# Attention on one core: value products in halves of 256 columns, and one head's row maximum taken from half the keys plus a relu

## The reference, cut to what matters

```python
Q = (hs @ q_w + q_b).reshape(B, S, H, HD).transpose(0, 2, 1, 3)
K = (hs @ k_w + k_b).reshape(B, S, H, KPH).transpose(0, 2, 1, 3)
V = (hs @ v_w + v_b).reshape(B, S, H, KPH).transpose(0, 2, 1, 3)
scores = jnp.einsum('bhsk,bhtk->bhst', Q[..., :KPH], K) / math.sqrt(KPH)
attn = jax.nn.softmax(scores, axis=-1)
ao = jnp.einsum('bhst,bhtv->bhsv', attn, V)
```

## Time and profile before

| what | value |
|---|---|
| median of three executions | 4021.08 us |
| the profiled execution | 3990.48 us |
| its span, first to last instruction | 3988.9 us |
| mean granted TensorE clock | 0.922 of full speed |
| TensorE busy with products | 3377.5 us (85%) |
| VectorE busy | 3155.0 us (79%) |
| ScalarE busy | 2370.5 us (59%) |
| attention: first score product to last | 1926.56 to 3272.01 us |

### The profile page before, as it was taken

One profiled execution on the slowest core, in us unless ns is written; L12 is line 12 of the kernel. 1 busy time (PEld: TensorE's weight loads), 2 busy tenths in 40 slices (PEclk: granted clock), 3 DMA queues, 4 the chain that ended last, 5 costly groups with the idle time before them and its releaser, 6 DMA issues. The chain is left out here.

```text
span 3988.9 us, 64991 instructions
## 1 busy us (share of the span) xinstructions
PE 3377.5 (85%) x19711; PEld 2058.5 (52%) x19712; DVE 3155.0 (79%) x4214; ACT 2370.5 (59%) x4325; POOL 1366.7 (34%) x953
## 2 busy tenths in 40 slices
PE   8969898996669799797999999999999976299950
PEld 6745455553458688795333333333333324189940
DVE  7869999997866566477899999999999935277868
ACT  6668888886955433210577777777777761033323
POOL 7859998994014454301000000000000005744520
PEclk9989999998889899997799999999999996599975
DMA  7854444544869632394122323223223115222258
GB/s 262 283 187 164 159 163 166 179 146 166 280 174 255 164 111 74 109 291 134 27 54 62 69 53 72 58 55 75 54 60 71 30 21 178 87 86 89 90 175 293
DMA packets 531451, 521.11 MB, mean 131 GB/s; under 512 B 84784, under 2 KB 441264, under 8 KB 531040
## 3 DMA queue, kind: packets, MB, share of 16 engines
q1 hardware_dynamic: 517248, 480.45, 41.0%
q0 software_dynamic: 13952, 37.74, 2.7%
HBM read 301.15 MB, written 215.71 MB: 130 GB/s over the span
## 5 line engine op out<-in xcount | busy, mean ns | idle before, releaser
L2395 DVE TENSOR_REDUCE at_top<-at_psM 128x1 f32<-128x1024 f32 x1024 | 1205.1, 1218 | 101.5 <-PE at_psM L2254 99.8
L2363 ACT ACTIVATE at_probs<-at_psS 128x512 f32<-128x512 f32 x2048 | 1061.0, 603 | 286.0 <-PE at_psS L2280 286.0
L2280 PE MATMUL at_psS<-at_q,at_k 64*128 64x512 f32 x2048 | 803.4, 471 | 8.2 <-ACT at_probs L2363 8.1
L2254 PE MATMUL at_psM<-at_k,at_q 62*128 62x512 f32 x2048 | 704.9, 454 | 41.3 <-DMA at_vraw<-scratch_vf 22.0
L655 POOL TENSOR_TENSOR sc_prod<-sc_state,sc_c_row 128x1024 f32<-128x1024 f32 x256 | 648.8, 2564 | 84.1 <-DVE sc_state L806 72.2
L2254 PEld LDWEIGHTS at_psM<-at_k,at_q 62*128 62x128 f32 x2048 | 313.1, 190 | 621.4 <-DVE at_top L2395 539.3
L806 DVE TENSOR_TENSOR_SCAN sc_state<-sc_dec,sc_psI 128x1024 f32<-128x1024 f32 x256 | 574.2, 2276 | 43.6 <-PE sc_psI L727 34.0
L2293 PE MATMUL at_psV<-at_probs,at_v 128*32 128x512 f32 x4096 | 546.3, 605 | 0.0
L738 PE MATMUL sc_psY<-sc_prod,sc_ident 128*128 128x512 f32 x1024 | 480.5, 599 | 15.2 <-DVE sc_y L792 15.2
L2221 POOL COPY at_v<-at_vraw 128x256 f32<-128x256 f32 x32 | 12.8, 401 | 1249.4 <-DMA at_vraw<-scratch_vf 1166.6
L2280 PEld LDWEIGHTS at_psS<-at_q,at_k 64*128 64x128 f32 x2048 | 337.7, 184 | 170.3 <-ACT at_probs L2363 160.4
(11 more groups left out here) (409 smaller groups left out, 4904.4 us busy)
## 6 DMA issues: line engine op xcount, KB each, us to landing
sc_c_row<-scratch_bc SPq DMA_DIRECT2D x128, 512.0 KB, 3.7
scratch_xs<-at_zeros SPq DMA_DIRECT2D x140, 264.0 KB, 4.7
sc_b_row<-scratch_bc SPq DMA_DIRECT2D x32, 512.0 KB, 5.0
ec_y<-scratch_ys SPq DMA_DIRECT2D x32, 512.0 KB, 6.1
ex_x<-scratch_xs SPq DMA_DIRECT2D x39, 264.0 KB, 3.3
si_x<-in_x SPq DMA_DIRECT2D x16, 512.0 KB, 5.6
scratch_xn<-si_xn SPq DMA_DIRECT2D x16, 512.0 KB, 6.2
scratch_x_t<-si_xT SPq DMA_DIRECT2D x16, 512.0 KB, 3.1
```

Of the source, the lines that this page charges most:

```text
L2254: ins = pe.matmul(psM[t % 2][:, half * TILE:(half + 1) * TILE], rows_of(q4[j], h, 0, MAXROW)[:, c * P:(c + 1) * P], rows_of(k4[j], h, 0, M ...
L2280: pe.matmul(psS[v % 3][:], rows_of(k4[j], h, 0, GROUP)[:, c * P:(c + 1) * P], rows_of(q4[j], h, 0, GROUP)[:, half * TILE:(half + 1) * TILE ...
L2363: act.activation(probs[:, slot(j, v), :], psS[v % 3][:], ACT.Exp).then_inc(act_done, 1)
L2395: dve.tensor_reduce(top[j % 2][:, h, c:c + 1], psM[t % 2][:], AX.X, ALU.max, negate=True).then_inc(maxed, 1)
```

## The change

The value products of a group are cut into two halves of 256 columns, and one half is issued after each step in place of a whole group after every second one (`values`, `values_after`). Where a group is the last of its eight (`last_keys`), both halves are still issued together, after an odd step, and the even step behind it gets none.

Of the four heads of a quad, one (`DIFF_HEAD`, the tiles with t % 4 = 3) gets its row maximum in another way. With a the scores of a query against the first 512 keys and b those against the last 512, max(a, b) = b + relu(a - b). TensorE makes a - b in a `psS` bank with two accumulated products, against the first keys and against negated last keys `kn` (`difference`), two tiles ahead; ScalarE takes the relu of it into `mag` (`raised`); TensorE makes b alone in `psM`; VectorE adds the two and takes the maximum over 512 columns in one instruction (`tensor_tensor_reduce`, `maximum`). GpSimd negates the keys (`negative_keys`), once per unit. The entries of the `psS` banks are numbered ahead in one list, where a difference is an entry like a score: 9 entries for four steps instead of 8.

Besides, the clears of the operands are shared between VectorE (units 0 and 1) and GpSimd (2 and 3), the loads of a unit wait for that unit's clears alone, `ones` is cleared and copied later, `cleared.make` moves to the end of GpSimd's prologue, and loops of SP and GpSimd are written out.

The core of the diff:

```diff
-    turn_entry = TURN + 1
-    bank_at = dict(zip(at_slot, range(BANKS)))
-    NE = BANKS + 1
-    OPEN = 4
+    RING, PART = 24, TILE // 2
+    DIFF = 3
+    DIFF_HEAD = HEADS[DIFF]
+    score_at, diff_at, turn_at, entries = {}, {}, {}, 0
+    for v, t in [(0, t) for t in range(MT)] + [(1, t) for t in range(LEAD)]:
+        if t % QUAD == 1:
+            diff_at[v, t + 2], entries = entries, entries + 1
+    turn_at[0], entries = entries, entries + 1
+    for u in range(UNITS):
+        for s in range(MT):
+            for n in (2 * s, 2 * s + 1):
+                score_at[u, n], entries = entries, entries + 1
+                if n == TURN and u + 1 < UNITS:
+                    turn_at[u + 1], entries = entries, entries + 1
+            v, t = u + 1 + (s + LEAD) // MT, (s + LEAD) % MT
+            if v < UNITS and t % QUAD == 1:
+                diff_at[v, t + 2], entries = entries, entries + 1
     COLLECTED = (18 + LEAD, FIRST + LEAD)
...
+        kn = [m.sb(f"kn{j}", [MAXROW, TILE], F32R) for j in range(NQ)]
+        mag = [m.sb(f"mag{k}", [P, TILE]) for k in range(2)]
...
-                    sp.wait_ge(ready_made, 2 * j + 3)
+                    sp.wait_ge(zeroed[j], 2)
                     m.settle(sp)
                     load(0, j)
+                sp.wait_ge(ones_made, 1)
+                m.settle(sp)
+                for j in range(NQ):
                     for group in range(2):
                         dst = k4[j][GROUP * group + MAXROW:GROUP * (group + 1), :, :].bitcast(F32)
                         sp.dma_start(dst, ones[:]).then_inc(ones_in, 16)
...
-                cleared.make(pool)
+                for j in range(2, NQ):
+                    pool.memset(k4[j][:].bitcast(F32), 0.0).then_inc(zeroed[j], 1)
+                    pool.memset(q4[j][:].bitcast(F32), 0.0).then_inc(zeroed[j], 1)
...
+                def negative_keys(b, j):
+                    pool.wait_ge(loaded[j], (b + 1) * 16 * LOADS)
+                    pool.tensor_scalar(kn[j][:], rows_of(k4[j], DIFF_HEAD, 0, MAXROW)[:, TILE:T].bitcast(F32), -1.0, None,
+                                       ALU.mult).then_inc(kn_ready[j], 1)
...
-                def maxima(u, j, t, half):
-                    h, c = tile_of(t)
-                    if half == 0:
-                        if t > 1:
-                            pe.wait_ge(maxed, u * MT + (t - 1))
-                        elif not isinstance(u, int) or u:
-                            pe.wait_ge(maxed, u * MT + t - 1)
-                    ins = pe.matmul(psM[t % 2][:, half * TILE:(half + 1) * TILE],
+                def maxima(u, t, half):
+                    j, (h, c) = u % NQ, tile_of(t)
+                    if t % QUAD == DIFF and half == 0:
+                        return
+                    if half == (1 if t % QUAD == DIFF else 0) and u * MT + t > 1:
+                        pe.wait_ge(maxed, u * MT + t - 1)
+                    at = 0 if t % QUAD == DIFF else half
+                    ins = pe.matmul(psM[t % 2][:, at * TILE:(at + 1) * TILE],
                                     rows_of(q4[j], h, 0, MAXROW)[:, c * P:(c + 1) * P],
                                     rows_of(k4[j], h, 0, MAXROW)[:, half * TILE:(half + 1) * TILE], start=True, stop=True)
                     if half == NHALF - 1:
                         ins.then_inc(scored, 1)
...
+                def free(e):
+                    if e >= 3:
+                        pe.wait_ge(act_done, e - 2)
+                def difference(u, t):
+                    j, (h, c), e = u % NQ, tile_of(t), diff_at[u, t]
+                    free(e)
+                    pe.wait_ge(kn_ready[j], u // NQ + 1)
+                    query = rows_of(q4[j], h, 0, MAXROW)[:, c * P:(c + 1) * P]
+                    pe.matmul(psS[e % 3][:], query, rows_of(k4[j], h, 0, MAXROW)[:, 0:TILE], start=True, stop=False)
+                    pe.matmul(psS[e % 3][:], query, kn[j][:], start=False, stop=True).then_inc(keyed, 1)
...
-                def values(u, j, g):
-                    half, c = g // KC, g % KC
-                    pe.wait_ge(act_done, u * NE + (at_slot[4 * g + 3] + 2))
-                    if c == 0:
-                        pe.wait_ge(sums_ready, u * NHALF + (half + 1))
-                    if g == 0:
-                        pe.wait_ge(v_ready, u + (2 * NQ + 1))
+                def values(group, part):
+                    u, g = group // GROUPS, group % GROUPS
+                    j, half, c = u % NQ, g // KC, g % KC
+                    cols = slice(part * PART, (part + 1) * PART)
+                    if part == 0:
+                        pe.wait_ge(act_done, score_at[u, 4 * g + 3] + 1)
+                        if c == 0:
+                            pe.wait_ge(sums_ready, u * NHALF + (half + 1))
+                        if g == 0:
+                            pe.wait_ge(v_ready, u + (2 * NQ + 1))
                     for n, h in enumerate(KEYED):
-                        last = pe.matmul(psV[32 * h:32 * h + 32, :], v4[j][:, c, h, :], probs[:, slot(j, at_slot[4 * g + n]), :],
-                                         start=(c == 0), stop=(c == KC - 1))
-                    last.then_inc(summed, 1)
-                def step(u, j, b, s, last_unit, second_last):
-                    tile = s + LEAD
-                    ahead, t = 1 + tile // MT, tile % MT
-                    more = not (last_unit or (second_last and ahead == 2))
-                    mj, mb = (j + ahead) % NQ, b + (j + ahead) // NQ
+                        last = pe.matmul(psV[32 * h:32 * h + 32, cols], v4[j][:, c, h, :], probs[:, slot(u, 4 * g + n), cols],
+                                         start=(c == 0 and part == 0), stop=(c == KC - 1 and part == 1))
+                    if part == 1:
+                        last.then_inc(summed, 1)
+                def values_after(at):
+                    group = (at - 3) // 2
+                    if group < 0:
+                        return
+                    last_keys = group % KC == KC - 1
+                    if at % 2:
+                        values(group, 0)
+                    if at % 2 == 0 and not last_keys or at % 2 and last_keys:
+                        values(group, 1)
...
+                        scores(u, n)
+                        if n == TURN and u + 1 < UNITS:
+                            turn(u + 1)
+                    if more and t % QUAD == 1:
+                        difference(v, t + 2)
...
+                            pe.wait_ge(top_in[u % NQ], (u // NQ + 1) * 16 * QUAD)
+                        step(u, s)
+                        values_after(u * MT + s)
+                for at in range(UNITS * MT, UNITS * MT + 2):
+                    values_after(at)
...
+                def raised(u, t):
+                    e, k = diff_at[u, t], t // QUAD % 2
+                    act.wait_ge(keyed, e + 1)
+                    if u * MT + t >= 2 * QUAD:
+                        act.wait_ge(maxed, u * MT + t + 1 - 2 * QUAD)
+                    act.activation(mag[k][:], psS[e % 3][:], ACT.Relu).then_inc(act_done, 1)
...
-                dve.memset(ones[:], 1.0).then_inc(ready_made, 1)
-                for j in range(NQ):
-                    dve.memset(k4[j][:].bitcast(F32), 0.0).then_inc(ready_made, 1)
-                    dve.memset(q4[j][:].bitcast(F32), 0.0).then_inc(ready_made, 1)
-                dve.memset(top2[:], 0.0).then_inc(ready_made, 1)
...
+                for j in range(2):
+                    dve.memset(k4[j][:].bitcast(F32), 0.0).then_inc(zeroed[j], 1)
+                    dve.memset(q4[j][:].bitcast(F32), 0.0).then_inc(zeroed[j], 1)
+                dve.memset(ones[:], 1.0).then_inc(ones_made, 1)
+                dve.memset(top2[:], 0.0).then_inc(top2_made, 1)
...
+                def maximum(u, t):
+                    h, c = HEADS[t % QUAD], t // QUAD
+                    at = top[u % 2][:, h, c:c + 1]
+                    if t % QUAD != DIFF:
+                        dve.wait_ge(scored, u * MT + (t + 1))
+                        dve.tensor_reduce(at, psM[t % 2][:], AX.X, ALU.max, negate=True).then_inc(maxed, 1)
+                        return
+                    dve.wait_ge(act_done, diff_at[u, t] + 1)
                     dve.wait_ge(scored, u * MT + (t + 1))
-                    h, c = HEADS[t % QUAD], t // QUAD
-                    dve.tensor_reduce(top[j % 2][:, h, c:c + 1], psM[t % 2][:], AX.X, ALU.max, negate=True).then_inc(maxed, 1)
...
-                def minus_max(u, j):
+                    raised = mag[t // QUAD % 2]
+                    dve.tensor_tensor_reduce(raised[:], psM[t % 2][:, 0:TILE], raised[:], -1.0, 3e38, ALU.add, ALU.min,
+                                             at).then_inc(maxed, 1)
```

More of the change, by code:

```diff
@@ L2182, in _ @@
                         sp.dma_start(dst, ones[:]).then_inc(ones_in, 16)
-                maxima_rows(0, 0, 0)
-                def sequence(b, final):
-                    for j in range(NQ):
[L2187 to L2194, removed]
```

(66 more changed lines are left out.)

133 lines of the change are left out of this document (49 added, 84 removed).

## The result

The kernel before takes 4020.51 us (median of four executions), the changed one 4072.28 us (four, 4070.74 to 4075.22): a ratio of 1.0129, 95% interval 1.0111 to 1.0146. The change costs 51.8 us; 36.6 were predicted.

What follows compares the result with a forecast made beforehand. The prediction took a 2.61 us loop of three banks, ScalarE and TensorE as the bound; steps +42.0 us and prologue -5.4 made +36.6, so 4021.1 became 4057.7 us. Its own range was 4035 to 4080, the full range 3986 to 4110.

Steps and rivals of the forecast that it cites:

- The bound before: Loop of two steps before the change, through three score banks, ScalarE and TensorE: 2.61 us, VectorE not in it.
- A half then costs 0.43 + 0.15, taken as 0.57: Value half on TensorE: 0.43 us of streaming, which halves, plus 0.15 of loading and emptying, which does not.
- Rival 1: Value halves: loading and emptying shrink with the block, a half takes 0.50 us, kernel 3986 us; chance 0.24.
- A plain step is thus 0.34 + 0.31 + 0.57 = 1.22 us: TensorE's step without a difference: load to second product, then to the values' load, then a half; 1024 make 1249.3 us.
- The difference, 0.46: Two more TensorE products with nothing beside them, 2 x 0.23 us, for 246 differences: 113.2 us.
- Turn and last keys, 0.45 and 0.17: Extra us at each of 31 unit turns (14.0 us) and 64 places with both halves together (10.9 us).
- ScalarE: Nine entries in four steps: 4.4 of 5.34 us, hidden; the difference's bank frees 0.46 us into its step.
- rival 3: Difference steps: the ring of three banks binds again, TensorE waits for ScalarE, 60 us more, 4118 us; chance 0.14.
- rival 4: ScalarE's relu: table loads each time, +657 us, kernel 4715 us; chance 0.03.
- Rival 2: Maxima's first load pulled under the values' stream, hiding 0.11 us a step, 113 us: kernel 3945 us; chance 0.04.
- Prologue, -5.4: Before the steps: `ones` cleared later, reductions start at 1867.0 instead of 1872.39, saving 5.4 us.
- Carrying the sum from the profile to the median: Whole kernel: median 30.6 us above the profiled execution, that difference carried over, so 4021.1 + 36.6 = 4057.7 us.

Runs made afterwards that it cites:

- halves_only: The changed kernel without the differences, one value half after each step, every tile reduced over 1024 scores: 3953.32 us, ratio 0.9832 to the kernel before.
- quarters: The kernel with halves and no differences, its value groups cut further into quarters of 128 columns, one after each score: 4286.31 us (one execution).
- one_product: The changed kernel with the second product of each difference, the one with the negated keys, left out: 4009.03 us, ratio 0.9973 to the kernel before.
- diff_only: The changed kernel with whole value groups after odd steps and the differences kept: 4195.75 us, ratio 1.0439 to the kernel before.
- neither: The changed kernel with halves and differences both undone, the new prologue and written-out loops kept: 4017.38 us, ratio 0.9993 to the kernel before.
- before_again: The kernel before, unchanged, run again for a second profile: 4020.90 us.

## Why the prediction was right, point by point

- **The bound before** (a loop of the three banks and not VectorE): right. `halves_only` keeps all 1024 reductions and still wins 66 us. VectorE was not far behind, though: there it is a limit too.
- **"A half then costs 0.43 + 0.15, taken as 0.57":** 0.57 in every kernel with halves, and the quarters confirm both parts. Rival 1, the half at half price, falls. (The half at which the change would break even was put at 0.537; 0.57 less 36.6 / 1024 is 0.534.)
- **"A plain step is thus 0.34 + 0.31 + 0.57 = 1.22 us":** 1.23. The block of maxima and scores is 0.66 and not 0.65. This is the mis-sized term: 1024 x 0.01 = 10.2 us, two thirds of the 15.2 us by which the sum was short. Starts read to 0.01 us carry that much when they are multiplied by 1024. The steps by the measured terms: 1024 x 1.23 + 246 x 0.46 + 31 x 0.46 + 64 x 0.17 = 1397.9 us; measured 1397.3.
- **The difference, 0.46:** 0.46 (1.69 against 1.23), by `one_product` 0.23 for each product, and in the steps 112.9 us in all (1397.3 - 1284.4) where 113.2 was the sum; the times differ by 119.
- **Turn and last keys, 0.45 and 0.17:** 0.47 and 0.17.
- **ScalarE:** the difference loads 0.45 into its step, where 0.46 was worked out for its bank, and its waits are 10.4 us in all, not the 60 of rival 3. Between 2000 and 3200 us no score waits longer than the gap of 0.41 except behind the last keys, as the prediction asked. But it had no slack at this place: the bank was free just as the array was, the working could not have told 0.46 from a little more, and that it fell on the right side was in part luck. In `diff_only`, where no half stands between, it falls on the wrong one.
- **The relu:** 605 ns, like an exponential of 596. No table load appears; rival 4 falls.
- **VectorE:** 689 ns where 0.69 to 1.4 was the range, rest 9.5 of 50 us where 9 or more was forecast. What it saved bought nothing.
- **GpSimd and SP:** the negated keys take 1484 ns each, and no instruction waits for them in the waits between 2000 and 3200 us.
- **Rival 2,** weight loads under the values' stream: the load of maxima stands 0.57 behind the half's in every plain step. It falls.
- **Prologue, -5.4:** the reductions start at 1867.77 (predicted 1867.0), the first score comes 5.2 earlier, or 5.7 counted from the first clear. Both profiles of before take 73.2 us for that stretch, `neither` and `halves_only`, which have no differences, 68.1 and 68.2, the changed kernel 67.5: the 10 differences in it cost no more time than the shorter reductions give back.
- **Carrying the sum from the profile to the median:** a difference of the two was right to carry, since the 30 us lay in the routing. Of the 15.2 us missed, 10 are the step's; about 5 are left. Against `before_again` the routing is 4.7 us longer (260.2 against 255.5), which is as much as it differs among the other runs (255.5 to 260.5), so whether the change has a part in it is not settled.

## What to carry to other kernels

Before an engine is relieved, draw the loop of waits that sets the step and see whether that engine is in it: here VectorE looked like the bound by every total, and the loop ran through three banks, ScalarE and TensorE. Work that was moved to the engine that sets the pace was paid in full, except where it was put beside products that use the other half of the array's rows (0.24 instead of 0.46). Cutting work in pieces paid here while it broke a wait longer than the changeover it added: halves won 66 us, quarters lost 333 against them.

## What was not expected of the hardware

The instruction that adds and takes a maximum at once leaves a second row on VectorE, a read of its accumulator (2502.38 in the timeline, 0.08 us), beside its own 0.69. And one stage, the routing, took 228.1 us in one execution and 255.5 in another of the same kernel, 27.4 us apart, where the four timed executions of it lie within 5.8 us.
